# A graph convolution whose indirect gathers take 127 edges each instead of 128

## The reference

```
gcn(h, W, b) = segment_sum((h @ W)[src] * weight[:, None], dst) + b
h   = elu(gcn(layernorm(x), W1, b1))
x   = x + elu(gcn(h, W2, b2))
H   = gelu(layernorm(x) @ Wf + bf)                # 256 -> 1024
p   = softmax(H @ Wg + bg)                        # 8 experts, the largest one is taken
x   = x + p[e] * (H @ Wd[e] + bd[e])              # e = argmax p
```

## Time and profile before

| | us |
|---|---|
| median of 3 runs (lowest, highest) | 4681.98 (4681.29, 4687.24) |
| span of the profiled execution | 4687.7 |
| first layer, start of first to start of last gather | 89.9 to 2056.4 |
| second layer, the same | 2075.8 to 4075.2 |
| one gather on POOL, median, first and second layer | 0.946, 0.946 |

### The profile page before, as it was taken

One profiled execution on the slowest core, in us unless ns is written; L12 is line 12 of the kernel. 1 busy time (PEld: TensorE's weight loads), 2 busy tenths in 40 slices (PEclk: granted clock), 3 DMA queues, 4 the chain that ended last, 5 costly groups with the idle time before them and its releaser, 6 DMA issues.

```text
span 4687.7 us, 84720 instructions
## 1 busy us (share of the span) xinstructions
PE 3478.1 (74%) x21458; PEld 3215.9 (69%) x21459; DVE 1979.0 (42%) x6592; ACT 1116.6 (24%) x1692; POOL 3267.9 (70%) x3405
## 2 busy tenths in 40 slices
PE   2766676676666666667877777777777777859999
PEld 1666666665666665657777777777777777748887
DVE  8333333333333333334454454445444444573333
ACT  4111111111111111113333333333333333311111
POOL 5777777777777777767777777777777777524444
PEclk7766666667666666669999999999999999889999
DMA  8333333333333333334444444444444444335554
GB/s 278 113 113 112 113 111 112 113 112 112 113 111 113 112 113 112 113 95 128 145 139 144 144 137 143 145 144 139 141 145 139 142 143 145 116 127 169 180 175 150
DMA packets 266657, 627.24 MB, mean 134 GB/s; under 512 B 63397, under 2 KB 135034, under 8 KB 265922
## 3 DMA queue, kind: packets, MB, share of 16 engines
q0 software_dynamic: 170688, 492.87, 36.6%
q1 hardware_dynamic: 95362, 129.30, 7.9%
HBM read 519.25 MB, written 103.63 MB: 133 GB/s over the span
## 4 chain that ended last, share of the span: by engine, by line
PE 40%; issue 21%; POOL 15%; DVE 11%; DVEq 5%; DMA 5%; ACT 2%; POOLq 0%; ACTq 0%; SPq 0%
PE pA L1164 23%; POOL rows L537 15%; PE pA L1286 8%; PE pB L1202 4%; DMA rows<-xn_scratch,idx 3%; DVE S L847 2%; PE pZ L1174 1%; ACT L653 1%; DVE work L929 1%; DVEq L359 1%; PE pC L1276 1%; PE pB L1276 1%; DVE work L924 1%; DVEq L876 1%; DVE aggT L886 1%
## 5 line engine op out<-in xcount | busy, mean ns | idle before, releaser
L1164 PE MATMUL pA<-S,rows 128*128 128x96 f32 x12544 | 2040.8, 337 | 716.0 <-DVE S L847 314.5
L1164 PEld LDWEIGHTS pA<-S,rows 128*128 128x128 f32 x12544 | 1966.6, 249 | 834.3 <-issue 421.7
L537 POOL DMA_INDIRECT rows<-h_scratch,idx x1568 | 1502.3, 958 | 516.5 <-issue 492.5
L537 POOL DMA_INDIRECT rows<-xn_scratch,idx x1568 | 1490.2, 950 | 485.2 <-issue 458.1
L886 DVE TENSOR_TENSOR aggT<-aggT,pA 128x192 f32 x784 | 277.3, 354 | 2061.0 <-PE pA L1164 1421.4
L625 ACT ACT_TABLE_LOAD x196 | 251.5, 1283 | 3002.5 <-DVE aggT L886 3000.4
L847 DVE TENSOR_SCALAR S<-iota_w,tdst,twgt 128x96 f32<-128x96 f32 x3152 | 843.9, 343 | 5.5 <-issue 2.6
L1174 PE MATMUL pZ<-wg,stage 128*128 128x256 f32 x784 | 295.2, 514 | 252.6 <-ACT stage L625 252.6
L1202 PE MATMUL pB<-work,w 128*128 128x128 f32 x3232 | 389.2, 279 | 33.2 <-DVE work L929 33.2
L1202 PEld LDWEIGHTS pB<-work,w 128*128 128x128 f32 x3232 | 370.1, 192 | 42.0 <-DVE work L929 42.0
L1286 PE MATMUL pA<-aggT,work 128*128 x1680 | 381.7, 380 | 0.0
(11 more groups left out here) (175 smaller groups left out, 2107.9 us busy)
## 6 DMA issues: line engine op xcount, KB each, us to landing
pay_scratch<-work SPq DMA_DIRECT2D x98, 512.0 KB
rows<-xn_scratch,idx POOLq DMA_INDIRECT x1568, 2.8
rows<-h_scratch,idx POOLq DMA_INDIRECT x1568
h_scratch<-work SPq DMA_DIRECT2D x98, 128.0 KB
pay_scratch<-work SPq DMA_DIRECT2D x98, 128.0 KB, 2.5
work<-in_x_dram SPq DMA_DIRECT2D x97, 128.0 KB
rows<-in_x_dram SPq DMA_DIRECT2D x24, 512.0 KB, 5.2
xn_scratch<-rows SPq DMA_DIRECT2D x24, 512.0 KB, 5.9
```

The costliest lines, as they stand in the source:

```text
L537: pool.indirect_dma_start(rows[:, s, t, :], None, source, bass.IndirectOffsetOnAxis(at, 0))\
L1164: last = mm(to[:, k * W:(k + 1) * W], rows[:, slot, t, k * P:(k + 1) * P], Sx[:, t, :], start=(t == 0), stop=(t == T - 1))
```

## The change

Each gather takes LANES = 127 edges, on partitions 0 to 126, and a group is GE = 508 edges; the number of rounds follows from it. Indices, S, tables and products use 127 lanes. pB is cleared once. The constants iota_w and tnum become views of iota_p.

```diff
--- before.py
+++ after.py
@@ -52,7 +52,8 @@
     KC = C // P
     KH = HID // P
     T = 4
-    GE = T * P
+    LANES = 127
+    GE = T * LANES
     W = 96
     SLOTS = 8
     HALF = SLOTS // 2
@@ -134,7 +135,6 @@
         flip = sb("flip", [P, P])
         ones = sb("ones", [P, P])
         before = sb("before", [P, P])
-        iota_w = sb("iota_w", [P, W])
         stats = sb("stats", [P, LNB, T, 6])
         mv = sb("mv", [P, LNB, T, 2])
         std = sb("std", [P, LNB, T])
@@ -159,8 +159,9 @@
         LG = sb("LG", [P, NB + DEPTH, NX])
         epsc = sb("epsc", [P, 1])
         prefer = sb("prefer", [P, NX])
-        tnum = sb("tnum", [P, NT])
         iota_p = sb("iota_p", [P, P])
+        iota_w, tnum = iota_p[:, 0:W], iota_p[:, 0:NT]
+        assert NT <= P
         node = sb("node", [P, NB])
         lists = sb("lists", [P, 2, NT])
         ids = sb("ids", [P, RING], i32)
@@ -227,7 +228,7 @@
         s_held = {e.engine: sem(f"held_{n}") for n, e in
                   (("sync", nc.sync), ("pool", nc.gpsimd), ("dve", nc.vector), ("act", nc.scalar))}
         s_const = sem("constants_ready")
-        NCONST = 12
+        NCONST = 10
         s_rows_clear = sem("edge_rows_padded")
         s_rows = sem("edge_rows_loaded")
         s_w = sem("weights_loaded")
@@ -503,9 +504,9 @@
                                pattern=[[1, P]], channel_multiplier=-1).then_inc(s_const, 1)
             for t in (tdst, twgt, tsrc):
                 pool.memset(t[:, :, NG:TBL], 0.0).then_inc(s_tbl_clear, 1)
-            for to, pattern, base, per_lane in ((iota_w, [[1, W]], 0, 0), (woff, [[W, KWIN + 1]], 0, 0),
+            for to, pattern, base, per_lane in ((woff, [[W, KWIN + 1]], 0, 0),
                                                 (prefer, [[-1, NX]], NX, 0), (iota_p, [[1, P]], 0, 0),
-                                                (tnum, [[1, NT]], 0, 0), (node, [[P, NB]], 0, 1)):
+                                                (node, [[P, NB]], 0, 1)):
                 pool.iota(to[:, :], pattern, base=base, channel_multiplier=per_lane,
                           allow_small_or_imprecise_dtypes=True).then_inc(s_const, 1)
             pool.memset(zeros[:, :, :], 0.0).then_inc(s_const, 1)
@@ -533,8 +534,8 @@
                             hold(pool, s_idx[layer], 2 * i + s // HALF + 1)
                         hold(pool, s_mm[layer], g + 1)
                         for t in range(T):
-                            at = idx[:, s // HALF, s % HALF, t:t + 1]
-                            pool.indirect_dma_start(rows[:, s, t, :], None, source,
+                            at = idx[0:LANES, s // HALF, s % HALF, t:t + 1]
+                            pool.indirect_dma_start(rows[0:LANES, s, t, :], None, source,
                                                     bass.IndirectOffsetOnAxis(at, 0))\
                                 .then_inc(s_gath[layer][s], 16)
 
@@ -582,8 +583,9 @@
                 cnt = P if c < GCH - 1 else TAILG
                 act.wait_ge(s_tT, n + 1)
                 at = NG - c * P - cnt
-                act.activation((tdst, tsrc, twgt)[n // GCH][:, :, at:at + cnt],
-                               pB[:, (n % 2) * 512:(n % 2 + 1) * 512].rearrange("p (t g) -> p t g", t=T)[:, :, 0:cnt],
+                act.activation((tdst, tsrc, twgt)[n // GCH][0:LANES, :, at:at + cnt],
+                               pB[0:LANES, (n % 2) * 512:(n % 2 + 1) * 512]
+                               .rearrange("p (t g) -> p t g", t=T)[:, :, 0:cnt],
                                ACT.Copy).then_inc(s_tcopied, 1)
 
 
@@ -775,7 +777,8 @@
 
             def stage_idx(layer, h, half):
 
-                v.tensor_copy(idx[:, half, :, :], tsrc[:, :, bass.ds(h * HALF, HALF)].rearrange("p t g -> p g t"))\
+                v.tensor_copy(idx[0:LANES, half, :, :],
+                              tsrc[0:LANES, :, bass.ds(h * HALF, HALF)].rearrange("p t g -> p g t"))\
                  .then_inc(s_idx[layer], 1)
 
             dve.wait_ge(s_tcopied, 3 * GCH)
@@ -828,6 +831,7 @@
             tc.then(v.memset(work[:, :], 0.0))
             tc.then(v.memset(pZ[:, 0:C], 0.0))
             tc.then(v.memset(pT[:, 0:C], 0.0))
+            tc.then(v.memset(pB[:, :], 0.0))
             v.memset(bmv[:, :], 1.0).then_inc(s_regs, 1)
             for sm in (s_zb[0], s_zb[1], s_xn2, s_hb, s_elu[0], s_elu[1], s_var2, s_xTc, s_lg):
                 dve.sem_inc(sm, 1)
@@ -844,8 +848,9 @@
 
                 dve.wait_ge(s_mm[layer], g + (SLOTS - 1))
                 for t in range(T):
-                    last = v.tensor_scalar(S[:, half, t, :], iota_w[:, :], tdst[:, t, bass.ds(g, 1)],
-                                           twgt[:, t, bass.ds(g, 1)], ALU.is_equal, ALU.mult)
+                    last = v.tensor_scalar(S[0:LANES, half, t, :], iota_w[0:LANES, :],
+                                           tdst[0:LANES, t, bass.ds(g, 1)], twgt[0:LANES, t, bass.ds(g, 1)],
+                                           ALU.is_equal, ALU.mult)
                 last.then_inc(s_S[layer], 1)
 
             def overflow(layer, g, base):
@@ -854,12 +859,12 @@
                 with dve.If(ws < we):
                     with dve.Fori(ws, we) as w:
                         k = within(w - ws + 1, 1, KWIN)
-                        v.tensor_scalar(cur[:, :], tdst[:, :, bass.ds(g, 1)].rearrange("p t g -> p (t g)"),
-                                        woff[:, bass.ds(k, 1)], None, ALU.subtract).then_inc(s_ovc[layer], 1)
+                        v.tensor_scalar(cur[0:LANES, :], tdst[0:LANES, :, bass.ds(g, 1)].rearrange("p t g -> p (t g)"),
+                                        woff[0:LANES, bass.ds(k, 1)], None, ALU.subtract).then_inc(s_ovc[layer], 1)
                         dve.wait_ge(s_ovc[layer], w + 1)
                         for t in range(T):
-                            last = v.tensor_scalar(Sov[:, t, :], iota_w[:, :], cur[:, t:t + 1],
-                                                   twgt[:, t, bass.ds(g, 1)], ALU.is_equal, ALU.mult)
+                            last = v.tensor_scalar(Sov[0:LANES, t, :], iota_w[0:LANES, :], cur[0:LANES, t:t + 1],
+                                                   twgt[0:LANES, t, bass.ds(g, 1)], ALU.is_equal, ALU.mult)
                         last.then_inc(s_ovS[layer], 1)
                         dve.wait_ge(s_ovmm[layer], w + 1)
                         at = within(base + k * W, 0, N - 1)
@@ -1145,7 +1150,7 @@
                     need(pe, s_tcopied, n - 1)
                     for t in range(T):
                         at = (n % 2) * 512 + t * P
-                        last = mm(pB[:, at:at + cnt], rowtable[0:cnt, c, t * P:(t + 1) * P],
+                        last = mm(pB[0:LANES, at:at + cnt], rowtable[0:cnt, c, t * LANES:(t + 1) * LANES],
                                   flip[0:cnt, P - cnt:P], start=True, stop=True)
                     last.then_inc(s_tT, 1)
                     n += 1
@@ -1161,7 +1166,7 @@
 
                 for k in range(KC):
                     for t in range(T):
-                        last = mm(to[:, k * W:(k + 1) * W], rows[:, slot, t, k * P:(k + 1) * P], Sx[:, t, :],
+                        last = mm(to[:, k * W:(k + 1) * W], rows[0:LANES, slot, t, k * P:(k + 1) * P], Sx[0:LANES, t, :],
                                   start=(t == 0), stop=(t == T - 1))
                 last.then_inc(semaphore, 1)
 
```

## The result

The kernel after takes 9910.4 us (median of 4 runs, 9907.6 to 9912.1), the kernel before beside it 4684.6 us: a ratio of 2.1155, 95% interval 2.1125 to 2.1185. The forecast was 4759 us, its range ended at 5500.

What follows compares the result with a forecast made beforehand. POOL's 1.25 us gather beat was taken to bound both layers, the second jointly with the PE/DVE chain. Terms 80 - 4 + 1 = +77 us, carried to the median, gave 4759 us; range 4320 to 5500, the forecast's own 4730 to 4785.

Steps and rivals of the forecast that it cites:

- What bounds the kernel: Both message-passing layers: POOL writing gather descriptors sets the first alone, the second together with the PE/DVE chain.
- POOL's beat: In both layers a gather of about 0.95 us plus 0.30 us pause, 1.25 us from start to start.
- the sign that the prediction had named against it: A second layer that shrinks with a faster beat would mean its PE/DVE chain was no bound, only paced by POOL.
- the first of that half: Second layer: gather 672, starting 0.30 us after DVE ended staging that half's indices, read as showing both chains bind.
- More gathers: Per layer 1600 gathers instead of 1568, in 50 rounds instead of 49; 64 more at 1.25 us, +80 us.
- without further ticks: Second layer: the PE/DVE chain grows only 24 us, node blocks staying 98, so POOL's 40 us count.
- A gather of 127 rows: POOL's price per gather: bounds -24 us if paid per row, 0 if fixed; -4 us taken.
- Landing: Gathered rows' arrival, 2.8 us now, about 7 later if on single engines in turn; covered, so 0, up to +10 us.
- the same instruction and columns, so 0: S, indices, products and tables on 127 lanes were to cost nothing.
- a dearer gather: Rival, chance 0.16: POOL writes all rows into one ring by another loop; 5000 to 6260 us, middle 5400.
- A cheaper gather: Rival, chance 0.37: POOL's gather gets shorter if time goes by rings or the 16-way split; 4507 us, range 4340 to 4670.
- One engine for all: Rival, chance 0.03: every 127-row gather goes to the same DMA engine, beat 7.2 us, about 23800 us.

Runs made afterwards that it cites:

- groups508_all128: Kernel after (groups of 508 edges), but gathers, S and products on 128 lanes, lane 127 with weight 0: 4788 us, ratio to before 1.0217.
- groups512_x400c: Groups of 512 edges on 128 lanes, but 50 rounds, the last nine groups empty: 4802 us, ratio to the kernel before 1.0254.
- before_products127: Kernel before with the edge products alone on 127 rows of the array instead of 128: 4720 us, ratio to before 1.0077.
- gather128_use127: Kernel after with the gathers alone put back to 128 rows, the rest on 127 lanes: 4829 us, ratio to before 1.030.
- before_rows127: Kernel before with the gather alone cut to 127 rows: 9721 us.

## Why the prediction was wrong, point by point

- **What bounds the kernel**: right. Both layers go at POOL's beat, and the beat's 0.30 us stayed. A change of the gather's price by 1602 ns came out of the time whole, 5126 of 5222 us. That the second layer's PE/DVE chain is a bound beside it held for small steps (4 of 20 us with 112 rows, 14 of some 77 with 126); with 16 rows the layer shrank by 99 us, the sign that the prediction had named against it, and this stays unexplained. One reading under it was off: 672 = 42 x 16 gathers start up to 2929.71, so the gather called "the first of that half" is the last of its half. The indices staged at 2929.41 were wanted 1.55 us later, at 2930.96, and the 0.30 us before 2929.71 is the beat, whatever releaser stands beside it. (The three castings start 24.2 and 16.9 us apart, not 17.0.)
- **More gathers**: the number right, the size short. Fifty rounds cost 47 to 53 us in the first layer and 60 to 63 in the second, not 40 and 40 (groups508_all128, groups512_x400c). The weak step was "without further ticks": their number stays 98, but behind the groups without edges two halves have two ticks each, and POOL waits for indices there (1.6, 4.6, 10.6 and 1.2 us). Its waits for indices rose from 45.9 to 90.9 us over the span. What makes the ticks bunch in just these halves is not shown.
- **A gather of 127 rows**: this step failed, and it decides all. "By the rows alone a step from 128 to 127 that only shortens a loop costs nothing": -4 us was taken, +5126 measured. POOL's time goes by the rows of the engine that gets most, 8 before and 127 after, at 13 ns each. The mistake was in the bounds. The prediction saw from the packets that 128 rows leave in 16 equal shares and that 127 can't, and still bounded the price by the row count (-24 to 0). The packets held the other bound: eight rows per engine before, up to 127 on one. It would have been a wide one: no row of before parts the 946 ns into a fixed part and steps, and with all of it in eight steps a gather of 127 would take 15 us. The range to 5500 was thus too narrow for what was known, and the forecast's own 4730 to 4785 all the more.
- **Landing**: forecast near 10 us in the case of one engine at a time, measured 8.0; the 18 GB/s taken for one engine were some 25. It never mattered: PE waits for rows, but POOL never for a free buffer or for indices.
- **127 lanes "the same instruction and columns, so 0"**: wrong for PE. The matmuls' columns are the same, but the clock granted falls from 0.66 and 0.91 to 0.57 and 0.87 (before_products127), 35 to 41 us. In the kernel after this can't be read, as PE waits there anyway.
- **The rivals**: "a dearer gather" (0.16) came nearest, with all rows in one ring, but "by another loop", and sized it by the scatter, 0.08 to 0.47 us instead of 1.6. What fits the runs is the same loop with 127 steps instead of 8, since 16 to 122 rows lie on the same 13 ns a step. "A cheaper gather" fell, and its remark that the same 16 completions are posted was the sign against it: all 16 engines get their packets whatever the rows. "One engine for all" fell, as landing and beat show.

## What to carry to other kernels

Choose the number of rows of an indirect gather by its largest divisor k up to 16, so that rows/k is small, not by its size. Here, with rows of 1 KB, 112 rows are as cheap as 128, 120 and 126 cost 4 to 5% more, 122 (twice a prime) and 127 (a prime) cost 1.8 and 2.7 times as much on POOL. Where a size on a hardware queue loses its divisor, take the extreme split, everything in one share, into the range, wide as it gets, or measure one transfer first; the packets per transfer tell which split it was. And one row less in a product isn't free even where the instruction takes the same columns; read the granted clock.

## What the runs showed of the hardware that was not expected

The filler packets: a gather on one engine still sends packets to all 16, 528 instead of 48, with 4 bytes for each row that an engine doesn't get. The DVE's part: with the longer gathers S took 1025 ns in the mean of the second layer instead of 344, and the layernorm's tensor_scalar 1477 instead of 480, while additions stayed at 355 and 354. After, and then before:

```profile
L851 DVE TENSOR_SCALAR S<-iota_p,tdst,twgt 127x96 f32<-127x96 f32 x1596 | 958.6, 1025 | 13.1 <-issue 12.0
L943 DVE TENSOR_SCALAR work<-work,bmv,bstd 128x256 f32<-128x256 f32 x97 | 143.2, 1477 | 3.5
L891 DVE TENSOR_TENSOR aggT<-aggT,pA 128x192 f32 x399 | 141.6, 355 | 2856.4 <-PE pA L1169 2485.1 <-issue 371.3
```

```profile
L847 DVE TENSOR_SCALAR S<-iota_w,tdst,twgt 128x96 f32<-128x96 f32 x1548 | 414.7, 344 | 3.1 <-issue 0.6
L886 DVE TENSOR_TENSOR aggT<-aggT,pA 128x192 f32 x388 | 137.3, 354 | 882.6 <-PE pA L1164 487.1 <-issue 395.4
L938 DVE TENSOR_SCALAR work<-work,bmv,bstd 128x256 f32<-128x256 f32 x97 | 46.5, 480 | 3.5
```

It is not the 127 lanes: gather128_use127 has the same S at 343 ns in the mean, and before_rows127 has 1044 on 128 lanes. It comes with the length of the gather on POOL beside it: the longest S is 564, 872, 1260 and 2129 ns beside gathers of 946, 1292, 1672 and 2548 (128, 124, 122 and 127 rows). The Trainium skill, page "SBUF — State Buffer", section "Who interferes with whom", says that a tensor_scalar can take both of DVE's port pairs, one of which is GpSimd's, and that whoever comes second waits for the other's whole instruction; the trace agrees that S waits for POOL, with S instructions of up to 2129 ns. That the wait is for the whole instruction it doesn't show: 2129 less the usual 324 are 1.8 us, 0.74 us short of the gather's 2.55, and at 122 and 124 rows the longest wait is as much short. It cost no time here, because DVE had it: its additions waited 5251 us for PE over the span.
